# A graph kernel on one core: the first layer norm moves into the projection stage that reads it

## What is computed

```
h = jnp.maximum(_layernorm(x, axis=-1), 0.0)
x = x + _L0_gnn_ref(h, adj, W_seq, a1, a2, W_out, b_out)
...
seq = (x @ W_seq).reshape(N, H, DH)               # N 2048, H 16, DH 32
score1 = jnp.einsum('nhd,d->hn', seq, a1)
score2 = jnp.einsum('nhd,d->hn', seq, a2)
scores = leaky_relu(score1[:, :, None] + score2[:, None, :])
scores = scores + (1.0 - adj)[None, :, :] * MASK_VAL
attn = jax.nn.softmax(scores, axis=-1)            # adj is 2048 x 2048, f32
```

## Time and profile before

| | us |
|---|---|
| median of 3 runs (lowest, highest) | 4285.27 (4284.05, 4287.05) |
| span of the profiled execution, first to last instruction | 4283.1 |
| busy in the span: PE, DVE, ACT, POOL | 3570.2, 3536.2, 2616.4, 1413.4 |
| start of the norm stage's last work on DVE, and its end | 36.84, 37.53 |
| first matmul of the projection stage | 43.97 |
| first DMA of the attention stage | 151.50 |

### The profile page before, as it was taken

The page is one execution under the profiler, slowest core; times in us unless marked ns, Lnnn a source line. Parts: engine busy times, 40 slices in busy tenths (PEclk is TensorE's granted clock), DMA queues, the critical chain, the costliest instruction groups (busy, mean ns, idle before and its releaser), DMA issues. The chain is left out here.

```text
span 4283.1 us, 55860 instructions
## 1 busy us (share of the span) xinstructions
PE 3570.2 (83%) x20136; PEld 2068.0 (48%) x20136; DVE 3536.2 (83%) x5848; ACT 2616.4 (61%) x3072; POOL 1413.4 (33%) x1417
## 2 busy tenths in 40 slices
PE   6889989879888838687887889899997967788887
PEld 3689989534344414333343344577773422333333
DVE  4699999679999996799999925799984169999996
ACT  3677777559888875588897823454543344444442
POOL 0343200017778794399988811000001100000000
PEclk9999999989998969899898899999998988888888
DMA  4611100211110100511101034000002111111110
GB/s 151 246 32 27 32 27 22 84 46 50 43 45 23 37 17 23 170 40 42 30 20 42 18 125 151 22 19 19 19 9 74 69 64 59 44 49 45 45 44 15
DMA packets 160244, 228.80 MB, mean 53 GB/s; under 512 B 85137, under 2 KB 96288, under 8 KB 154672
## 3 DMA queue, kind: packets, MB, share of 16 engines
q1 hardware_dynamic: 148592, 191.33, 13.8%
q0 software_dynamic: 11376, 33.76, 2.2%
HBM read 158.48 MB, written 66.47 MB: 53 GB/s over the span
## 5 line engine op out<-in xcount | busy, mean ns | idle before, releaser
L1695 DVE SCALAR_TENSOR_TENSOR junk<-expd,mid 128x2048 bf16<-128x2048 f32 x440 | 1036.4, 2356 | 13.8
L579 ACT ACTIVATE steepz<-s1b,thr_h 128x1024 bf16<-128x1024 f32 (+1 forms) x832 | 733.5, 942 | 394.1 <-DVE mask L646 380.9
L732 PE MATMUL acc<-V,mask 128*128 128x198 bf16 (+1 forms) x5504 | 745.8, 274 | 100.4 <-DVE mask L646 51.5
L1595 ACT ACTIVATE junk_s<-expd,nmid 128x2048 bf16<-128x2048 f32 x264 | 528.8, 2003 | 129.6 <-POOL nmid L1655 116.1
L732 PEld LDWEIGHTS acc<-V,mask 128*128 128x128 bf16 x5504 | 478.7, 99 | 163.7 <-DVE mask L646 56.5
L1598 ACT ACTIVATE junk_s<-expd,nmid 128x2048 bf16<-128x2048 f32 x264 | 528.0, 2000 | 0.0
L2140 PE MATMUL psS<-KT,qs 64*128 64x512 f32 x1024 | 367.5, 728 | 130.7 <-DVE m L2253 125.5
L646 DVE TENSOR_TENSOR mask<-steepz,adjT 128x1024 bf16<-128x1024 bf16 (+1 forms) x832 | 438.4, 565 | 18.5 <-ACT steepz L579 8.6
L739 PE MATMUL acc<-V,adjT 128*128 128x99 bf16 (+1 forms) x5504 | 452.5, 220 | 0.0
L739 PEld LDWEIGHTS acc<-V,adjT 128*128 128x128 bf16 x5504 | 368.7, 99 | 49.6 <-issue 1.0
L1467 PE MATMUL psX<-parts,block 128*128 128x512 bf16 x1536 | 364.6, 394 | 10.4 <-DMA block<-adj_dram 10.4
(11 more groups left out here) (306 smaller groups left out, 5941.0 us busy)
## 6 DMA issues: line engine op xcount, KB each, us to landing
rows<-in_adj_dram SPq DMA_DIRECT2D x32, 1024.0 KB, 5.3
s1b<-sT_dram SPq DMA_DIRECT2D x32, 512.0 KB, 3.8
block<-adj_dram SPq DMA_DIRECT2D x32, 512.0 KB, 4.5
adj_dram<-adjT POOLq DMA_DIRECT2D x4, 2048.0 KB, 20.8
rel_table<-zeros POOLq DMA_DIRECT2D x64, 128.0 KB, 19.9
y_dram<-yo SPq DMA_DIRECT2D x32, 256.0 KB, 2.0
step_dram<-xo SPq DMA_DIRECT2D x32, 256.0 KB, 2.0
A<-step_dram SPq DMA_DIRECT2D x8, 1024.0 KB, 13.6
```

The costliest lines, as they stand in the source:

```text
L579: act.activation(steepz[:, m % RELUS, :], s1b[:, q % 4, :], ACT.Relu, bias=thr_h[:, u, 1, j:j + 1], scale=STEEP).then_inc(relu_ready, 1)
L732: mm = pe.matmul(acc[:, c % 2, i // TB, o:o + 2 * W], mask[:, j % RING, tile(i)], V[:, u, j, 0:2, :].rearrange("p s w -> p (s w)"), start= ...
L1595: act.activation(junk_s[:, 0, :], expd[:, slot[i], :], ACT.Relu, bias=col(nmid, i), accum_out=col(above, i)).then_inc(sums_ready, 1)
L1695: link(dve.scalar_tensor_tensor(junk[:, :], e, col(mid, i), e, ALU.is_gt, ALU.mult, accum_out=col(mass, i)))
```

## The change

norm_stage is gone, and project_stage makes the norm itself, through RowNorm:

- x is loaded straight into `seq` (buffer A) and normed in place. The first of its four DMAs is issued ahead of `w`, the other three behind `w`; the first two loads of rows follow, then a1 and a2.
- DVE takes moments and scales in four groups of four tiles, `scale` of one group after the first moments of the next. The folding of a1 and a2 is spread: one of the 8 pieces behind each of the first 8 `turned(t)`.
- ACT does Relu with scale and bias, and also the copies of the turned tiles, which DVE did before.
- PE turns 4 tiles (AHEAD = 4) before the first matmul, and then two more behind the matmuls of each projected tile t = 0 to 5, ahead of `turn_rows(t)`.
- `psS` lies in the first bank of `psR` and no longer has its own.

```diff
+            norm = RowNorm(self, st, seq, tr)
+            AHEAD = 4
...
             def _(sp):
-                    for k in range(KD):
-                        sp.dma_start(w[:, k, :], w_dram[tile(k), :]).then_inc(w_in, 16)
+                load_x(0)
+                for k in range(KD):
+                    sp.dma_start(w[:, k, :], w_dram[tile(k), :]).then_inc(w_in, 16)
+                for c in range(1, 4):
+                    load_x(c)
+                load_rows(0)
+                load_rows(1)
...
             def _(dve):
+                for t in range(NT):
+                    if t % 4 == 0:
+                        dve.wait_ge(x_in[t // 4], 16)
+                    norm.moments(dve, link, t, seq[:, t, :])
+                    if t >= 4 and t % 4 == 0:
+                        norm.scale(dve, link, t // 4 - 1)
+                norm.scale(dve, link, NT // 4 - 1)
+                for t in range(ROWS_FIRST - 2):
+                    turned(t)
+                    if t < 2 * KD:
+                        fold(t)
...
             def _(act):
+                norm.root(act, 0)
+                relu(0)
+                relu(1)
+                relu(2)
+                norm.copy(act, 0)
+                relu(3)
+                for t in range(1, AHEAD):
+                    norm.copy(act, t)
+                for c in range(1, 4):
+                    norm.root(act, c)
+                relu(AHEAD)
+                relu(AHEAD + 1)
                 for t in range(NT):
+                    for n in range(AHEAD + 2 * t, min(AHEAD + 2 * t + 2, NT)):
+                        norm.copy(act, n)
+                        if n + 2 < NT:
+                            relu(n + 2)
+                    act.wait_ge(adj_in[t % 2], 16 * (t // 2 + 1))
...
             def _(pe):
                 def sequence(t):
+                    pe.wait_ge(norm.n_copied, t + 1)
...
                     mm.then_inc(seq_ready, 1)
-                    if adj_dram is not None:
-                        turn_rows(t)
+                    for n in range(AHEAD + 2 * t, min(AHEAD + 2 * t + 2, NT)):
+                        norm.turn(pe, n)
+                    turn_rows(t)
...
+                for t in range(AHEAD):
+                    norm.turn(pe, t)
                 for t in range(ROWS_AFTER):
                     sequence(t)
```

More of the change, by code:

```diff
@@ L200, in identity @@
                                 pattern=[[-1, P]], channel_multiplier=1))
[L203 to L275, removed]
-                    for k in range(KD):
-                        mm = pe.transpose(psT[:, t % 2, k, :], nat[:, t, tile(k)], self.ident[:, :])
-                    mm.then_inc(t_ready, 1)
@@ L330, in project_stage @@
-            block = st.enter_context(nc.Block())
[L332 to L336, removed]
+            adj_in = [self.sem(st, f"adj_in{c}") for c in range(2)]
+            cast = self.sem(st, "cast")
+            a_ready = self.sem(st, "a_ready")
+            a_copied = self.sem(st, "a_copied")
+            id_done = self.sem(st, "id_done")
@@ L338, in _ @@
+            AHEAD = 4
+            block = st.enter_context(nc.Block())
+            @block.gpsimd
+            def _(pool):
+                link = chain(pool, id_done)
+                self.identity(pool, link, self.ident)
+                self.identity(pool, link, ident16)
             @block.sync
             def _(sp):
[L340 to L345, removed]
-                        sp.dma_start(w[:, k, :], w_dram[tile(k), :]).then_inc(w_in, 16)
@@ L364, in _ @@
                 sp.dma_start(m2[:, :], g.top_dram[H:2 * H].partition_broadcast(P)).then_inc(m2_in, 16)
-                if adj_dram is not None:
-                    for t in range(ROWS_FIRST, NT):
-                        load_rows(t)
+                for t in range(ROWS_FIRST, NT):
+                    load_rows(t)
                 sp.wait_ge(sT_out, 16)
@@ L372, in _, with fold @@
                 link = chain(dve, dve_done)
[L374 to L383, removed]
+                def fold(n):
+                    k, i = n // 2, n % 2
+                    if n == 0:
+                        dve.wait_ge(w_in, 16 * KD)
+                        dve.wait_ge(a_in, 32)
+                    link(dve.tensor_tensor(prod[:, :].rearrange("p (h d) -> p h d", h=H),
+                                           w[:, k, :].rearrange("p (h d) -> p h d", h=H),
+                                           avec[:, i, :, :].to_broadcast([P, H, DH]), ALU.mult))
+                    ins = dve.tensor_reduce(w12[:, k, i, :], prod[:, :].rearrange("p (h d) -> p h d", h=H), AX.X, ALU.add)
+                    if n == 2 * KD - 1:
+                        ins.then_inc(w12_ready, 1)
+                    else:
+                        link(ins)
                 def turned(t):
@@ L389, in turned @@
                                         psA[:, half, :, :]).then_inc(a_copied, 1)
-                if adj_dram is not None:
-                    for t in range(ROWS_FIRST - 2):
-                        turned(t)
+                link(dve.memset(shift[:, :], SHIFT))
+                for t in range(NT):
[9 more added lines that the diff above has]
+                        fold(t)
                 dve.wait_ge(sT_copied, 4)
@@ L396, in _ @@
                 dve.wait_ge(s_ready, 1)
-                dve.tensor_copy(s[:, :, :, :].rearrange("p t i h -> p t (i h)"), psS[:, :, :]).then_inc(s_copied, 1)
+                dve.tensor_copy(s[:, :, :, :].rearrange("p t i h -> p t (i h)"), psS).then_inc(s_copied, 1)
                 dve.wait_ge(s_copied, 1)
[L399 to L403, removed]
-                    link(dve.reciprocal(self.rinv[:, :], deg[:, :]))
+                for t in range(ROWS_FIRST - 2, NT):
+                    turned(t)
+                dve.wait_ge(cast, NT)
+                link(dve.tensor_scalar(deg[:, :], deg[:, :], 1.0, 1e-12, ALU.add, ALU.max))
+                link(dve.reciprocal(self.rinv[:, :], deg[:, :]))
                 dve.wait_ge(m2_in, 16)
```

60 lines of the change are left out of this document (28 added, 32 removed).

## The result

| | before | changed |
|---|---|---|
| median of the runs (lowest, highest), 4 each | 4285.26 (4284.05, 4287.05) | 4301.68 (4296.23, 4309.29) |
| profiled execution: span | 4283.1 | 4294.5 |
| first projection matmul | 43.97 | 17.98 |
| start of the 32 passes into `psR` | 88.13 | 102.00 |
| first DMA of the attention stage | 151.50 | 166.54 |

The changed kernel is slower: 1.0039 times the time before (95% interval 1.0025 to 1.0053), 16.4 us on the medians. The profiled execution itself took 4296.23 us, 1.7 above its span.

A forecast was written before the change was run, and what follows sets the result against it. PE was taken as the pace from the first matmul (43.97) to `psR` (88.13). 33.6 + 57.2 + 5.0 + 6.9 = 102.7, 14.6 us later, plus 1.7 for low clock: +16.3, about 4302 us; range 4291 to 4310.

The forecast's parts named there:

- the ring: Tiles 1 to 5: PE waits for the cast, ACT for the turn; 9.45 us per tile at full clock against 4.38.
- Up to the first matmul: Norm of the first tiles: PE's first projection matmul at 17.9 us against 43.97, 26.1 us gained.
- Tile 0's own wait: Tile 0: last square root at 25.7, Relu 4 ends at 26.8, tile 1's matmuls start at about 33.6 us.
- The clock's part: Tiles 1 to 4: low clock after each PE wait adds 1.8 to 2.7 us per tile, taken as 2.3.
- The term of tile 5: Tile 5: no Relus behind it, 1.42 us less than the 11.75 of earlier tiles, given as 10.2.
- Tiles 6 and 7: Last two projected tiles: 5.0 us for tile 6, 6.9 for tile 7, which waits for the last folded piece.
- Low clock at `psR`: Passes into `psR` after a PE wait of 2.5 us: 0 to 3.4 us more, taken as 1.7.
- Behind it, as before: Everything after the passes into `psR`: unchanged, so the kernel is 16.3 us longer in all.
- PE as the pace: Rival for tiles 1 to 5: cast done during the matmuls, 5.24 us PE work per tile, `psR` at 71.1, 4268 us; chance 0.05.
- The clock that stays up: Rival for tiles 1 to 5: no low clock after waits, `psR` at 89.9, +1.8 us, 4287 us; chance 0.09.
- The clock that stays down: Rival: low clock in nearly the whole ring, 13.6 us per tile, `psR` at 112, 4311 us; chance 0.08.
- the shorter Relu of the bounds: ACT's Relus might take the plain activation's 0.53 us, 0.36 shorter per tile, 1.8 in all.

The follow-up runs named there:

- e2_pe_kept_busy: Changed kernel with 4 extra PE matmuls in each of tiles 0 to 5, ahead of the wait for the cast, result thrown away; 4297.86 us.
- e4: The changed kernel itself run once more, nothing edited; 4301.14 us.
- e5: Changed kernel, but all 16 tiles normed and turned before the first projection matmul, ACT alternating Relu and copy; 4270.74 us.
- e9: The kernel of e2_pe_kept_busy run once more; 4294.89 us.
- e1: Changed kernel with the cast of the adjacency rows ahead of the two copies and two Relus in ACT's list; 4270.6 us.
- e8: The kernel of e1 run once more; 4269.29 us.
- e10: e6_cast_first_all_fixes with the square roots of groups 2 and 3 one place earlier each; 4257.0 us.
- e6_cast_first_all_fixes: Changed kernel with cast ahead of copies, fold in the first 4 turned tiles, roots of groups 2 and 3 and scaling of group 0 moved; 4263.41 us.
- e3_fold_early: Changed kernel with two folded pieces behind each of the first 4 turned tiles instead of one behind each of the first 8; 4299.76 us.

## Why the prediction was right

The time forecast was 4302, measured 4301.7 and 4301.1, and the mechanism was the one forecast, the ring with a cast that has lost its cover and the clock that falls in each of its waits. Step by step:

- *Up to the first matmul*: forecast 17.9, measured 17.98. The second MB of x let DVE go on at 11.95 (forecast about 12.0), the first Relu began at 13.08 (13.2).
- *Tile 0's own wait*: the last root at 25.79 (25.7), turn 4 at 26.76 (26.8), tile 1 at 33.78 (33.6). Its matmuls took 4.71 and not 6.5, since the clock rose on the way; as forecast this hid behind the wait for Relu 4.
- *The ring*: 45.77, 56.88, 68.89, 80.38 and 89.60 give 12.0, 11.1, 12.0, 11.5 and 9.2 us for tiles 1 to 5, in sum 55.8 against 57.2. At the full clock it is 9.46 (e2_pe_kept_busy), forecast 9.45. The clock's part, 2.2 us per tile for 1 to 4, was taken at 2.3. The term of tile 5 was 1.0 too large (10.2; by its own working, 11.75 - 1.42, it would be 10.3): its matmuls ran at the low clock for a shorter while (84.51 - 80.38 = 4.13 us against the 5.0 to 5.4 of the earlier trace rows).
- *Tiles 6 and 7*: 5.5 and 6.9, forecast 5.0 and 6.9. `psR` at 102.00, forecast 102.7.
- *Low clock at `psR`*: 15.62 - 13.92 = 1.7, the value taken, and that it came is in part luck: behind the same wait of 2.32 us the passes took 15.6 us in four of seven profiles (the changed kernel, e4, e5, e9) and 13.92 in three (e1, e2, e8), and e2 and e9 are one kernel.
- *Behind it, as before*: 15.0 us later at the attention stage, forecast 16.3.

That the median met the number to 0.3 us is in part luck. The profile shows 15.0 us lost up to the attention stage, not 16.3, and the stages behind it took from 4128.0 (the changed kernel's profile) to 4141.9 us (e10's). The profiled execution of the changed kernel was only 11.4 us longer than that of before: attention took 630.1 against 632.6 us, and 807.7 against 810.5 passed from the first loads of the first top-p step to those of the second. What made the medians differ by 16.4 isn't shown.

The rivals: PE as the pace is what e1_cast_first shows, and it needs the other order, as was argued; 5.26 us per tile against the 5.24 that were worked out, and `psR` at 69.89 and 70.62 against 71.1. In that sum two misses met: tile 1 began at 30.96, not 33.6, since the cast of tile 0 went ahead of its copies as well, and took 6.7 us instead of 5.24. The clock that stays up is what e2_pe_kept_busy shows; it needs work in the gap. The clock that stays down did not come: it was back up within the matmuls of each tile, which took 4.3 to 5.8 us and not 6.5. For the Relu with scale and bias, ACT took 0.81 to 0.82 us in place (0.80 in the earlier trace rows), so the shorter Relu of the bounds did not come. The Trainium skill ("ScalarE: Activation LUTs", "What ACT_TABLE_LOAD costs") says that each operand of scale or bias that is read per partition adds about 93 ns to an ACTIVATE; this Relu has two of them, and the traces agree, with 0.80 us against 0.63 for the activation without them.

## What to carry to other kernels

When work is woven into a loop of two engines, what counts is not each engine's sum (PE 5.2 us and ACT 4.8 per tile here) but where the hand-overs stand in the two lists. An operation that needs nothing from this step (the cast) goes ahead of those that wait for this step's work on the other engine (the copies, which wait for the turns). Behind them both lie open, the copies and Relus and then the cast: 9.46 - 5.26 = 4.2 us per tile, and with the low clock after each wait 11.65 - 5.26 = 6.4. Check every list that something was moved past: the same mistake was in DVE's list in e6_cast_first_all_fixes (the turned copies behind a scaling, 3.3 us and a slow tile), and, in the changed kernel, in the place of the last folded piece.

## What was not expected of the hardware

The same 8192 matmuls of the attention stage took 629.6 to 640.2 us, at granted clocks of 0.96 down to 0.94, in kernels that don't differ there, and in two profiles of one kernel (631.4 and 639.4). The kernel before scattered likewise over the sessions, from 4276.87 to 4292.49 us in one of them, though its first four runs had lain within 3 us. A gain of 4 us in a stage (e3_fold_early) is plain in the profile of that stage and can't be seen in the medians. Whether a wait of PE costs clock varies too: after the wait of 2.95 to 3.97 us for the rows of tile 13, the next matmuls took 3.65 us in three of the fourteen profiles (e1, e2, e9) and 4.3 to 5.8 in the others, e8, the same kernel as e1, among them. Open is why the projection stages that ended 13.5 us earlier thanks to extra passes of PE gave only some 4 us; extra passes of PE in the kernel before did not raise its median.
